# Expert blocks of 128 rows instead of 256, their first layer in 16-bit halves that are prepared earlier, and resident biases

## The chip, the cores and the metric

One Trainium2 chip, one of its cores. The time is the device time of one execution in microseconds (us), as the median of the runs of one kernel. The engines are TensorE (PE, whose weight loads are listed as PEld), VectorE (DVE), ScalarE (ACT), GpSimd (POOL) and SyncE (SP, which here only issues DMAs and passes waits on).

## The reference

2500 nodes of 512 features pass a graph layer and then a layer of eight experts. Cut to what matters:

```python
x = x + gnn(_layernorm(x), edge_index)     # relu((h + segment_sum(h[src])) @ W1 + b1) @ W2 + b2
xt = _layernorm(x)
gate = softmax(xt @ Wg); topv, topi = top_k(gate, 2); topv = topv / (sum(topv) + 1e-06)
for e in range(8):                         # D = 512, H = 256
    h = gelu(xt @ W1[e] + b1[e])
    ye = h @ W2[e] + b2[e]
    out = out + ye * scores[:, e]          # scores is topv at the two chosen experts, else 0
x = x + out
```

All is float32. The node count, 80000 edges, and 2 experts for each node give 5000 (node, expert) rows for the experts.

## The kernel before

**Aggregation (to about 396 us).** The sum over edges is a matmul of node features with a matrix of edge counts. DVE builds one-hot rows for each of 125 windows of 20 nodes (`one_hots`: `hot_key`, `hot_lo`), PE multiplies them (`window`), ACT copies the counts out (`take_counts`), and PE multiplies the counts with the 16-bit halves of the features (`sums_tile`). An outer loop `for it in range(1, G + 1)` takes 25 windows a turn and lays in between them the second graph layer of an earlier group of 500 nodes (`mlp2` on PE; `logits_of`, `residual` and `residual_end` on DVE; `std2` on ACT; on POOL the low halves of the hidden rows and the sum of residual input and bias, `x_res`). DVE may be at most RING = 4 windows ahead of PE. All of it is one hand-written order per engine, in which every wait is on a semaphore. `residual_end` writes the normalised rows `xt` as float32, SP stores them to `xt_d` in DRAM.

**Routing (about 413 to 442 us).** DVE works out for each (node, expert) row a slot, so that each expert's rows fill whole blocks of B rows; PE spreads node numbers and scores over the slots. Experts hold different numbers of rows, so there are empty places. NB is the most blocks that there can be, and blocks behind the last real one are run through the same loops on all engines but PE, with rows that go to spare lines of the output.

**Blocks (from about 442 us).** POOL fetches each block's rows by indirect DMA (`gather`, 128 rows of 2 KB each) into one of XB places. PE turns them (`turn`, matmuls with an identity), ACT and DVE make the high and the low part of the turned rows (`turned_high`, `turned_low`; one buffer `xT_hi`, `xT_lo`), PE runs the first layer as three products (high by high, high by low, low by high), in two halves m of the 256 hidden columns; ACT applies Gelu with the bias (`he`), DVE makes the low half (`he_lo`), PE runs the second layer, again three products; DVE adds the expert's second bias (`y`), ACT multiplies by the score, POOL adds the rows to the output by an indirect DMA that accumulates (`add_rows`). In the source the order for block k is the same on each engine: on ACT Gelu of k, the turned rows of k + 1, then the score of k; on DVE `he_lo` of k, turned rows of k + 1, then `y` of k.

An accumulating DMA must not run beside another that touches the same output row. Rows of one expert are all different nodes, so SP's `let_add` holds POOL's adds back only where the expert changes: there it waits until the last adds have landed. For the first YB blocks it waits on every earlier one. SP also loads the expert's second bias for each block (`load_bias`).

Each expert's weights W1, W2 are loaded as float32 and split by ACT (`split_high`) and DVE (`split_low`) into high and low parts, partly before the blocks and partly in their first rounds.

Counted from the reference with its own inputs, the experts get 407, 291, 1018, 356, 656, 1545, 405 and 322 rows.

## Time and profile before

| what | value |
|---|---|
| median of 3 runs | 638.52 us (637.46 to 639.03) |
| the profiled execution's own time | 639.89 us |
| its span (first to last instruction shown) | 638.1 us |
| busy, share of the span | PE 87%, DVE 66%, ACT 48%, POOL 40% |
| granted TensorE clock, mean | 0.948 of full speed |
| matmuls of each kind in the experts' first layer | 192, that is 24 blocks of 8 |

The shares are means over three stages that differ: how full each engine is in the stage that a change touches is read from the table of stretches, and what ends last there from the order of instructions in time.

### The profile page before, as it was taken

Reading aid. Unit: us, or ns where it says so; the run is one execution under the profiler, and the core shown is the slowest. Engines: PE = TensorE matmul, PEld = TensorE weight load, DVE = VectorE, ACT = ScalarE, POOL = GpSimd, SP = SyncE. Lnnn points to the kernel's source line nnn. Section 1 sums busy time; section 2 is a strip of 40 time slices with the busy share of each in tenths; the row PEclk is TensorE's granted clock in tenths of the full one; section 3 lists DMA queues with packets and bytes.
Section 4 is the critical chain, followed back from the end, with each engine's and each line's share of the span. In section 5 each row is a group of like instructions: output and inputs, shape, how many; then the busy total and the mean of one; then the engine's idle time right before and its main releaser. Section 6 shows DMA issues by size and latency. Waiting matters only on the chain.

```text
span 638.1 us, 10741 instructions
## 1 busy us (share of the span) xinstructions
PE 555.6 (87%) x3852; PEld 437.3 (69%) x3853; DVE 419.2 (66%) x802; ACT 307.9 (48%) x582; POOL 252.2 (40%) x222
## 2 busy tenths in 40 slices
PE   5788879999999999999999999726999999999900
PEld 3688879667566666766766665725899998889800
DVE  4777888975588769867974321887766765545541
ACT  3464767442242251225222301658777776677761
POOL 4362323130080016004200610017567778788763
PEclk9999999999999999999999999956999999999965
DMA  8253300300021201310311132978678988999895
GB/s 254 86 146 95 104 1 1 77 1 1 2 65 49 85 15 49 97 50 3 96 51 50 50 97 66 336 251 263 134 167 181 191 187 191 192 209 187 178 183 67
DMA packets 40302, 71.91 MB, mean 113 GB/s; under 512 B 10313, under 2 KB 14545, under 8 KB 39714
## 3 DMA queue, kind: packets, MB, share of 16 engines
q0 software_dynamic: 12704, 29.22, 23.1%
q1 hardware_dynamic: 26103, 36.06, 19.0%
q10 hardware_dynamic: 1442, 5.94, 3.3%
q8 instruction: 32, 0.52, 0.3%
q14 instruction: 21, 0.17, 0.1%
HBM read 46.07 MB, written 26.69 MB: 114 GB/s over the span
## 4 chain that ended last, share of the span: by engine, by line
PE 53%; DMA 12%; POOL 10%; DVE 8%; ACT 7%; issue 6%; SPq 1%; ACTq 0%; POOLq 0%; DVEq 0%
PE psum L1429 27%; PE psum L1413 9%; PE psum L1466 7%; PE psum L1343 6%; POOL out_x L605 6%; DMA out_x<-y,target_i 6%; POOL xg L598 3%; DMA xg<-xt_d,token_i 2%; DMA b_now<-in_L_ffn_b 2%; DMA src_i<-in_src 2%; PE psum L1321 1%; ACT y L833 1%; DVE hot_key L1054 1%; DVE stat L867 1%; DVE hot_lo L1054 1%
## 5 line engine op out<-in xcount | busy, mean ns | idle before, releaser
L1054 DVE TENSOR_TENSOR hot_key<-iota_key,key_w 128x1200 f16<-128x1200 f16 x125 | 109.0, 872 | 48.7 <-PE psum L1413 47.8
L667 ACT ACTIVATE counts<-psum 128x400 bf16<-128x400 f32 x125 | 62.0, 508 | 155.9 <-PE psum L1413 155.7
L1429 PE MATMUL psum<-counts,z_hi 125*128 125x500 bf16 x400 | 101.8, 375 | 2.2 <-ACT h L691 1.6
L605 POOL DMA_INDIRECT out_x<-y,target_i x54 | 87.7, 1624 | 35.4 <-ACT y L833 12.8
L1429 PE MATMUL psum<-counts,z_lo 125*128 125x500 bf16 x400 | 101.5, 376 | 0.0
L570 POOL TENSOR_TENSOR h_lo<-h,h_hi 128x500 fp32r<-128x500 f32 x16 | 23.5, 1498 | 168.8 <-ACT h_hi L698 168.8
L1413 PE MATMUL psum<-hot_key,hot_lo 128*128 128x200 f16 x750 | 82.8, 250 | 4.9 <-DVE hot_lo L1054 3.5
L1054 DVE TENSOR_TENSOR hot_lo<-iota_lo,lo_w 128x768 f16<-128x768 f16 x125 | 84.5, 676 | 0.0
L1413 PEld LDWEIGHTS psum<-hot_key,hot_lo 128*128 128x128 f16 x750 | 66.0, 98 | 25.3 <-issue 5.3
L1429 PEld LDWEIGHTS psum<-counts,z_lo 125*128 125x128 f16 x400 | 39.3, 98 | 45.7 <-issue 1.1
L598 POOL DMA_INDIRECT xg<-xt_d,token_i x54 | 58.0, 1074 | 31.2 <-issue 16.2
L1268 DVE TENSOR_TENSOR he_lo<-he,he_hi 128x256 fp32r<-128x256 f32 x54 | 23.0, 426 | 64.6 <-ACT he L826 64.6
L1429 PEld LDWEIGHTS psum<-counts,z_hi 125*128 125x128 f16 x400 | 37.7, 98 | 30.2 <-SPq L447 1.9
L1562 PE MATMUL psum<-xT_hi,w_hi 128*128 128x256 f32 x192 | 54.3, 283 | 0.3 <-DVE xT_lo L1250 0.3
L1562 PE MATMUL psum<-xT_hi,w_lo 128*128 128x256 f32 x192 | 54.3, 283 | 0.0
L1562 PE MATMUL psum<-xT_lo,w_hi 128*128 128x256 f32 x192 | 54.3, 283 | 0.0
L833 ACT ACTIVATE y<-y,slot_score 128x512 f32<-128x512 f32 x54 | 36.0, 714 | 33.2 <-DVE y L1277 33.2
L573 POOL TENSOR_TENSOR x_res<-x_res,b_row 125x512 f32<-125x512 f32 x20 | 29.4, 1490 | 49.3 <-DMA x_res<-in_x 49.3
L557 POOL TENSOR_TENSOR z_lo<-z,z_hi 125x512 f16<-125x512 f32 x20 | 27.5, 1382 | 50.7 <-ACT z L660 50.7
L1573 PE MATMUL psum<-w_hi,he_hi 128*128 128x512 f32 x96 | 40.0, 416 | 3.2 <-DVE he_lo L1268 3.1
L1277 DVE TENSOR_TENSOR y<-psum,b_now 128x512 f32<-128x512 f32 x54 | 34.7, 684 | 10.1 <-DMA b_now<-in_L_ffn_b 6.6
L1466 PE MATMUL psum<-W_hi,h_hi 128*125 128x264 f32 (+1 forms) x128 | 37.9, 296 | 0.0
(259 smaller groups left out, 1149.6 us busy)
## 6 DMA issues: line engine op xcount, KB each, us to landing
w_raw<-in_L_ffn_W SPq DMA_DIRECT2D x16, 512.0 KB, 6.9
b_now<-in_L_ffn_b SPq DMA_DIRECT2D x27, 256.0 KB, 5.0
x_res<-in_x SPq DMA_DIRECT2D x20, 224.0 KB
out_x<-x SPq DMA_DIRECT2D x20, 224.0 KB
xt_d<-xt SPq DMA_DIRECT2D x20, 224.0 KB
W_raw<-in_L_gnn_W ACTq DMA_DIRECT2D x2, 1024.0 KB, 5.6
out_x<-in_x SPq DMA_DIRECT2D x1, 1536.0 KB, 9.5
x_in<-in_x ACTq DMA_DIRECT2D x3, 448.0 KB
```

Of the source, the lines that this page charges most:

```text
L598: pool.indirect_dma_start(out=xg[:, k % XB, i], out_offset=None, in_=xt_d[:, :], in_offset=bass.IndirectOffsetOnAxis(ap=token_i[:, 2 * k + ...
L605: pool.indirect_dma_start(out=out[:, :], in_=y[:, k % YB, i], in_offset=None, out_offset=bass.IndirectOffsetOnAxis(ap=target_i[:, 2 * k + ...
L667: act.activation(counts[:, it % 2, :, place:place + W], psum[:, WIN + w % 2, 0:MW].rearrange("p (w h) -> p h w", w=W), ACT.Copy).then_inc( ...
L833: act.activation(y[:, k % YB, i], y[:, k % YB, i], ACT.Copy, scale=slot_score[:, 2 * k + i:2 * k + i + 1])\
L1054: ins = dve.tensor_tensor(hot[:, w % RING].rearrange("p s (n two) -> p s n two", two=2), iota[:].rearrange("p (o n two) -> p o n two", o=1 ...
L1277: dve.tensor_tensor(y[:, k % YB, i], psum[:, 4 + i], b2_now[:, k % 2], ALU.add).then_inc(taken, 1)
L1343: ins = mm(psum[0:P, AGG + 2 * (t % 2) + b, 0:columns.stop - columns.start], x_[:, t % 2, k * P:(k + 1) * P], w_[:, k, columns], start=(n ...
L1413: ins = mm(psum[:, WIN + w % 2, a * MH:(a + 1) * MH], hot_lo[:, w % RING, k], hot_key[:, w % RING, k], start=(k == 0), stop=(k == SL - 1))
L1429: ins = mm(psum[:, AGG + c, 0:GN], half[:, t, c * 128:(c + 1) * 128], counts[0:P, g % 2, t], start=(t == 0 and n == 0), stop=(t == T - 1 a ...
L1466: ins = mm(psum[0:P, bank + b, 0:columns.stop - columns.start], h_[:, k, rows], w_[:, k, columns], start=(k == 0 and n == 0), stop=(k == K ...
L1562: ins = mm(psum[:, 2 + m, 0:B], w_[e][:, c, cols], x_[:, c], start=(c == 0 and i == 0), stop=(c == KC - 1 and i == 2))
L1573: ins = mm(psum[:, 4 + i, :], h_[:, m, i * 128:(i + 1) * 128], w_[e][:, m], start=(m == 0 and n == 0), stop=(m == HC - 1 and n == 2))
```

## The change

- B is 128 instead of 256. NB, by its formula, is 47 instead of 27. By the row counts above there are 4, 3, 8, 3, 6, 13, 4 and 3 = 44 blocks with rows (before 2, 2, 4, 2, 3, 7, 2 and 2 = 24), so 3 empty ones in both kernels.
- The rows `xt` are stored as two float16 halves, 1024 float16 a row, as many bytes as before. DVE (for the last five tiles ACT) writes the whole row and its high half, and POOL subtracts (`low_rows`); the store waits for POOL. `turn` now multiplies the gathered halves with a float16 identity, so ACT's copy `x_now` is gone, and the two halves of the turned rows are plain copies.
- W1 of each expert is scaled by powers of two, split into float16 halves and written to `up_d` in DRAM inside the third and fourth turn of the aggregation loop (it = 2 and 3, `up_slot`): per expert ACT makes sizes (`up_sizes`) and the high half (`up_high`), PE sums the sizes (`up_sums`), DVE scales (`up_scales`) and makes the low half (`up_low`). The loads and stores are on ACT's queue. The blocks' loading then takes both halves with one DMA, and only W2 is split there.
- Eight DMAs load all second biases (`b2_all`) before the blocks; ACT and DVE wait for them before block 0. `load_bias` is gone.
- Gelu is computed once for each half m; DVE copies the high part (`he_hi`) and subtracts.
- YB = 6 places for `y` of 128 rows instead of 3 of 256, XB = 8 places for gathered rows instead of 3 of 256. POOL puts `add_rows(k)` ahead of `gather(k + 8)`; before, a gather stood ahead of the add.
- The node numbers are spread by one table of 48 columns instead of two of 56; ACT's part in it is gone.

```diff
-B = 256
+B = 128
...
-XB = 3
-YB = 3
-PAD = 2 * YB * 128
-AHEAD = 5
+XB = 8
+YB = 6
+PAD = YB * 128
+AHEAD = 6
...
+        def up_slot(it, j, late=0):
+            turn, left = divmod(WG * (it - 2) + j - late, WG)
+            n = 4 * turn + (left - 7) // 5
+            return n if it >= 2 and left >= 7 and (left - 7) % 5 == 0 and 0 <= n <= NE else None
...
-                sp.dma_start(w1_raw[e][:], eW1[e].rearrange("(k p) h -> p k h", p=128)).then_inc(ew_in[e], 16)
+                sp.dma_start(w1_both[e][:], up_d[e]).then_inc(ew_in[e], 16)
...
+            for e in range(NE):
+                sp.dma_start(b2_all[:, e], eb2[e:e + 1, :].broadcast_to([128, D])).then_inc(S["eb_in"], 16)
...
+                if k == YB:
+                    sp.wait_ge(S["slots_known"], LANDINGS)
+                if k >= YB:
+                    landed = {a: sp.value_load(landed_i[0:1, a, k:k + 1], min_val=16, max_val=16 * NB)
+                              for a, back in ((0, 1), (1, YB - 1)) if k - back >= YB}
+                for back in range(1, YB):
+                    if k - back >= YB:
+                        sp.wait_ge(y_out[(k - back) % YB], landed[0 if (k - back) // YB == (k - 1) // YB else 1])
+                    elif k >= back:
+                        sp.wait_ge(y_out[(k - back) % YB], 16)
                 sp.sem_inc(S["rows_free"], 1)
...
+            def low_rows(g, q):
+                n = 4 * g + q
+                pool.wait_ge(S["xt_hi_ready"], n + 1)
+                pool.tensor_tensor(xt[:, q, 1], xt_whole[:, n % 2], xt[:, q, 0], ALU.subtract).then_inc(S["xt_ready"], 1)
...
             def add_rows(k):
                 pool.wait_ge(S["rows_free"], k + 1)
-                for i in range(2):
-                    pool.wait_ge(S["y_scaled"], 2 * k + i + 1)
-                    pool.indirect_dma_start(out=out[:, :], in_=y[:, k % YB, i], in_offset=None,
-                                            out_offset=bass.IndirectOffsetOnAxis(ap=target_i[:, 2 * k + i:2 * k + i + 1], axis=0),
-                                            compute_op=ALU.add).then_inc(y_out[k % YB], 16)
+                pool.wait_ge(S["y_scaled"], k + 1)
+                pool.indirect_dma_start(out=out[:, :], in_=y[:, k % YB], in_offset=None,
+                                        out_offset=bass.IndirectOffsetOnAxis(ap=target_i[:, k:k + 1], axis=0),
+                                        compute_op=ALU.add).then_inc(y_out[k % YB], 16)
...
+                act.wait_ge(S["xt_ready"], n - 1)
+                for part in (xt_whole[:, n % 2], xt[:, q, 0]):
+                    ins = act.activation(part, x2[:, q], ACT.Identity, scale=rstd2[:, n:n + 1], bias=ln2[:, q % 2, 9:10])
+                ins.then_inc(S["xt_hi_ready"], 1)
...
+            def up_high(e):
+                act.wait_ge(S["up_scaled"], 2 * e + 1)
+                if e >= 1:
+                    act.wait_ge(S["up_out"], 16 * e)
+                act.activation(up_split[:, 0], up_raw[:, e % 2], ACT.Copy).then_inc(S["up_rounded"], 1)
+            def next_up(e):
+                if e >= 1:
+                    act.wait_ge(S["up_scaled"], 2 * e)
+                    act.dma_start(up_d[e - 1], up_split[:]).then_inc(S["up_out"], 16)
+                if e + 1 < NE:
+                    load_up(e + 1)
...
-            act.wait_ge(S["at_tile_ready"], 1)
-            act.activation(token_part[:, :, 0], at_tile[:], ACT.Copy, scale=iota_p[:]).then_inc(S["parts_ready"], 1)
...
+            act.wait_ge(S["eb_in"], 16 * (NE + 1))
+            act.wait_ge(S["slots_known"], BLOCKS)
+            act.wait_ge(S["slots_known"], SCORES)
             for k in range(NB):
                 expert = act.value_load(expert_i[0:1, k:k + 1], min_val=0, max_val=NE - 1)
                 for m in range(HC):
                     act.wait_ge(S["up_done"], HC * k + m + 1)
                     if k >= 1:
                         act.wait_ge(S["he_ready"], HC * (k - 1) + m + 1)
-                    if k >= 1:
-                        act.wait_ge(S["down_done"], 2 * k)
-                    for half in (he_hi[:, m], he[:, m]):
-                        ins = act.activation(half, psum[:, 2 + m, 0:B], ACT.Gelu, bias=eb1_col[:, bass.ds(expert * HC + m, 1)])
-                    ins.then_inc(S["gelu_ready"], 1)
+                    at = bass.ds(expert * HC + m, 1)
+                    act.activation(he[:, m], psum[:, 2 + m, 0:B], ACT.Gelu, bias=eb1_col[:, at], scale=up_undo[:, at]).then_inc(S["gelu_ready"], 1)
                 turned_high(k + 1)
                 if k + 2 <= NB:
                     take_block(k + 2)
-                for i, taken in enumerate((S["y0_taken"], S["y1_taken"])):
-                    act.wait_ge(taken, k + 2)
-                    act.activation(y[:, k % YB, i], y[:, k % YB, i], ACT.Copy, scale=slot_score[:, 2 * k + i:2 * k + i + 1])\
-                       .then_inc(S["y_scaled"], 1)
+                act.wait_ge(S["y_taken"], k + 2)
+                act.activation(y[:, k % YB], y[:, k % YB], ACT.Copy, scale=slot_score[:, k:k + 1]).then_inc(S["y_scaled"], 1)
...
-                dve.tensor_scalar(xt[:, q], x2[:, q], ln2[:, q % 2, 6:7], rstd2[:, n:n + 1],
-                                  ALU.subtract, ALU.mult).then_inc(S["xt_ready"], 1)
+                if n >= 2:
+                    dve.wait_ge(S["xt_ready"], n - 1)
+                for part in (xt_whole[:, n % 2], xt[:, q, 0]):
+                    ins = dve.tensor_scalar(part, x2[:, q], ln2[:, q % 2, 6:7], rstd2[:, n:n + 1], ALU.subtract, ALU.mult)
+                ins.then_inc(S["xt_hi_ready"], 1)
...
+            def up_scales(n):
+                dve.wait_ge(S["up_summed"], n + 1)
+                if n < NE:
+                    dve.tensor_scalar(up_inverse[:], psum[:, SM, 0:H], LEAST, None, ALU.max).then_inc(S["up_read"], 1)
+                if n >= 1:
+                    dve.tensor_scalar(up_undo[:, HC * (n - 1):HC * n].bitcast(I32), psum[:, SM, H:H + HC].bitcast(I32),
+                                      -1, (254 - UP) << 23, ALU.mult, ALU.add).then_inc(S["up_read"], 1)
+                if n < NE:
+                    dve.wait_ge(S["up_read"], 2 * n + 1)
+                    step(dve.tensor_scalar(up_inverse[:].bitcast(I32), up_inverse[:].bitcast(I32), EXPONENT, EXPONENT,
+                                           ALU.bitwise_xor, ALU.bitwise_and))
+                    dve.tensor_tensor(up_raw[:, n % 2], up_raw[:, n % 2],
+                                      up_inverse[:].rearrange("p (o h) -> p o h", o=1).broadcast_to([128, KC, H]), ALU.mult)\
+                       .then_inc(S["up_scaled"], 1)
+            def up_low(e):
+                dve.wait_ge(S["up_rounded"], 2 * e + 2)
+                dve.tensor_tensor(up_split[:, 1], up_raw[:, e % 2], up_split[:, 0], ALU.subtract).then_inc(S["up_scaled"], 1)
...
-            split_low_up(0)
-            split_low_down(0)
-            split_low_up(1)
+                dve.wait_ge(S["turned"], 2 * k + 2)
+                dve.tensor_copy(xT_lo[:].rearrange("p c n -> p (c n)"), psum[:, 1]).then_inc(S["xT_ready"], 1)
+            split_low(0)
+            split_low(1)
...
+            dve.wait_ge(S["eb_in"], 16 * (NE + 1))
             for k in range(NB):
+                expert = dve.value_load(expert_i[0:1, k:k + 1], min_val=0, max_val=NE - 1)
                 for m in range(HC):
                     dve.wait_ge(S["gelu_ready"], HC * k + m + 1)
                     if k >= 1:
-                        dve.wait_ge(S["down_done"], 2 * k)
+                        dve.wait_ge(S["down_done"], k)
+                    step(dve.tensor_copy(he_hi[:, m], he[:, m]))
                     dve.tensor_tensor(he_lo[:, m], he[:, m], he_hi[:, m].bitcast(F32), ALU.subtract).then_inc(S["he_ready"], 1)
                 turned_low(k + 1)
-                if k < 2 * NE - 3:
-                    (split_low_down, split_low_up)[k % 2](1 + (k + 1) // 2)
-                dve.wait_ge(b2_in[k % 2], 16 * (k // 2 + 1))
+                if 2 <= k < NE:
+                    split_low(k)
                 if k >= YB:
-                    dve.wait_ge(y_out[k % YB], 32 * (k // YB))
-                for i, taken in enumerate((S["y0_taken"], S["y1_taken"])):
-                    dve.wait_ge(S["down_done"], 2 * k + i + 1)
-                    dve.tensor_tensor(y[:, k % YB, i], psum[:, 4 + i], b2_now[:, k % 2], ALU.add).then_inc(taken, 1)
+                    dve.wait_ge(y_out[k % YB], 16 * (k // YB))
+                dve.wait_ge(S["down_done"], k + 1)
+                dve.tensor_tensor(y[:, k % YB], psum[:, 4], b2_all[:, bass.ds(expert, 1)].rearrange("p o d -> p (o d)"), ALU.add).then_inc(S["y_taken"], 1)
...
+            def turn(k, place):
+                pe.wait_ge(S["x_now_ready"], k)
+                for h in range(2):
                     for c in range(KC):
-                        ins = pe.transpose(psum[:, i, c * 128:(c + 1) * 128], rows[:, i, c * 128:(c + 1) * 128], ident[:])
+                        rows = xg[:, place, h, c * 128:(c + 1) * 128]
+                        ins = mm(psum[:, h, c * 128:(c + 1) * 128], rows if place == 0 else rows.rearrange("p o d -> p (o d)"), ident16[:], start=True, stop=True)
...
-                    trio = [(w1_hi, xT_hi), (w1_lo, xT_hi), (w1_hi, xT_lo)]
+                    trio = [(0, xT_hi), (1, xT_hi), (0, xT_lo)]
                     for m in range(HC):
                         cols = slice(m * 128, (m + 1) * 128)
                         for c in range(KC):
-                            for i, (w_, x_) in enumerate(trio):
-                                ins = mm(psum[:, 2 + m, 0:B], w_[e][:, c, cols], x_[:, c], start=(c == 0 and i == 0),
+                            for i, (half, x_) in enumerate(trio):
+                                ins = mm(psum[:, 2 + m, 0:B], w1_both[e][:, half, c, cols], x_[:, c], start=(c == 0 and i == 0),
                                          stop=(c == KC - 1 and i == 2))
                         ins.then_inc(S["up_done"], 1)
-                    turn(k + 1)
+                    turn(k + 2, bass.ds((k + 1) & (XB - 1), 1))
                     trio = [(he_hi, w2_hi), (he_hi, w2_lo), (he_lo, w2_hi)]
                     for m in range(HC):
                         pe.wait_ge(S["he_ready"], k * 2 + (m + 1))
-                        for i in range(2):
-                            if m == 0:
-                                pe.wait_ge((S["y0_taken"], S["y1_taken"])[i], k + 1)
-                            for n, (h_, w_) in enumerate(trio):
-                                ins = mm(psum[:, 4 + i, :], h_[:, m, i * 128:(i + 1) * 128], w_[e][:, m],
-                                         start=(m == 0 and n == 0), stop=(m == HC - 1 and n == 2))
-                            if m == HC - 1:
-                                ins.then_inc(S["down_done"], 1)
+                        if m == 0:
+                            pe.wait_ge(S["y_taken"], k + 1)
+                        for n, (h_, w_) in enumerate(trio):
+                            ins = mm(psum[:, 4], h_[:, m], w_[e][:, m], start=(m == 0 and n == 0), stop=(m == HC - 1 and n == 2))
+                    ins.then_inc(S["down_done"], 1)
```

The order of DVE in the fourth turn of the aggregation loop, around one tile of `residual` and `residual_end` (`logits` to `ln` is the residual part, `hot_key` and `hot_lo` are one window's one-hot rows). Before:

```order
L1066 TENSOR_TENSOR logits<-psum,gate_in 125x8
L1068 MAX top<-logits 125x8
L1070 MAX_INDEX topi<-top,logits 125x8
L1079 TENSOR_TENSOR x<-psum,x_res 125x512
L1081 BN_STATS ln<-x 125x6
L1082 BN_AGGR ln<-ln 125x2
L1054 TENSOR_TENSOR hot_key<-iota_key,key_w 128x1200
L1054 TENSOR_TENSOR hot_lo<-iota_lo,lo_w 128x768
L1087 RECIPROCAL rstd<-ln 125x1
L1093 TENSOR_SCALAR xt<-x,ln,rstd 125x512
```

The same place in the changed kernel, on DVE again:

```order
L1114 TENSOR_TENSOR logits<-psum,gate_in 125x8
L1115 MAX top<-logits 125x8
L1116 MAX_INDEX topi<-top,logits 125x8
L1125 TENSOR_TENSOR x<-psum,x_res 125x512
L1127 BN_STATS ln<-x 125x6
L1128 BN_AGGR ln<-ln 125x2
L1162 TENSOR_TENSOR up_split<-up_raw,up_split 128x1024
L1102 TENSOR_TENSOR hot_key<-iota_key,key_w 128x1200
L1102 TENSOR_TENSOR hot_lo<-iota_lo,lo_w 128x768
L1133 RECIPROCAL rstd<-ln 125x1
L1142 TENSOR_SCALAR xt_whole<-x,ln,rstd 125x512
L1142 TENSOR_SCALAR xt<-x,ln,rstd 125x512
```

One subtraction of 1024 columns and a second normalised copy have come in. Three windows ahead of each such place DVE has this in the changed kernel, the scaling of one expert's W1:

```order
L1102 TENSOR_TENSOR hot_key<-iota_key,key_w 128x1200
L1102 TENSOR_TENSOR hot_lo<-iota_lo,lo_w 128x768
L1148 TENSOR_SCALAR up_inverse<-psum 128x256
L1150 TENSOR_SCALAR up_undo<-psum 128x2
L1154 TENSOR_SCALAR up_inverse<-up_inverse 128x256
L1156 TENSOR_TENSOR up_raw<-up_raw,up_inverse 128x1024
```

Before, nothing stood between the one-hot rows there. The second place is ACT's round of one block. Before (`TENSOR_LOAD` and `ISA` are register work, here the block's expert and the address of its bias):

```order
L818 TENSOR_LOAD expert_i
L818 ISA x2
L826 ISA
L826 ACTIVATE he_hi<-psum,eb_col 128x256
L826 ACTIVATE he<-psum,eb_col 128x256
L826 ISA
L826 ACTIVATE he_hi<-psum,eb_col 128x256
L826 ACTIVATE he<-psum,eb_col 128x256
L801 ACTIVATE xT_hi<-psum 128x4x128 x2
L810 ACTIVATE x_now<-xg 128x1024
L833 ACTIVATE y<-y,slot_score 128x512 x2
```

ACT's round of one block in the changed kernel:

```order
L871 TENSOR_LOAD expert_i
L871 ISA x2
L877 ISA
L877 ACTIVATE he<-psum,eb_col,up_undo 128x128
L877 ISA
L877 ACTIVATE he<-psum,eb_col,up_undo 128x128
L855 ACTIVATE xT_hi<-psum 128x512
L882 ACTIVATE y<-y,slot_score 128x512
```

The round is shorter, and the score of block k still stands ahead of Gelu of block k + 1.

## Rows read from the trace of the kernel before

**Rows 1.** Windows: busy us (and instructions) per engine in five stretches, granted clock, DMA.
```profile
175.00:233.00 58.00, 55.97 (x380) 36.69 (x378) 44.83 (x77) 17.26 (x36) 12.98 (x8) 1.00 0.20 59
233.00:291.50 58.50, 58.50 (x409) 40.09 (x407) 46.51 (x86) 17.86 (x37) 12.35 (x8) 1.00 0.18 54
413.00:442.50 29.50, 10.05 (x90) 9.30 (x90) 26.65 (x70) 20.54 (x25) 12.20 (x20) 0.54 0.85 261
487.00:598.00 111.00, 107.76 (x713) 97.75 (x713) 63.46 (x105) 79.57 (x146) 86.87 (x65) 1.00 0.91 191
604.50:638.00 33.50, 0.20 (x1) 0.00 (x0) 11.04 (x20) 14.84 (x28) 16.98 (x12) 0.58 0.76 129
```

**Rows 2.** Page, the chain that ended last, by engine.
```profile
PE 53%; DMA 12%; POOL 10%; DVE 8%; ACT 7%; issue 6%; SPq 1%; ACTq 0%; POOLq 0%; DVEq 0%
```

**Rows 3.** Timeline, two rounds of blocks: start, duration, engine, idle before and releaser.
```profile
591.17 1.29 DVE L1277 TENSOR_TENSOR y<-psum,b_now 128x512 f32<-128x512 f32 x2 [0.29 <-PE psum L1573]
...
591.89 1.34 ACT L833 ACTIVATE y<-y,slot_score 128x512 f32<-128x512 f32 x2 [0.91 <-DVE y L1277]
...
593.29 0.47 ACT L826 ACTIVATE he_hi<-psum,eb_col 128x256 fp32r<-128x256 f32 x1
...
593.66 0.47 ACT L826 ACTIVATE he<-psum,eb_col 128x256 f32<-128x256 f32 x1
...
594.16 0.42 DVE L1268 TENSOR_TENSOR he_lo<-he,he_hi 128x256 fp32r<-128x256 f32 x1 [1.70 <-ACT he L826]
...
601.71 0.47 PE L1573 MATMUL psum<-w_hi,he_hi 128*128 128x512 f32 x1
...
603.63 0.39 PE L1573 MATMUL psum<-w_hi,he_lo 128*128 128x512 f32 x1
...
604.16 1.29 DVE L1277 TENSOR_TENSOR y<-psum,b_now 128x512 f32<-128x512 f32 x2 [0.29 <-PE psum L1573]
```

**Rows 4.** Timeline of DVE and PE, routing to the first block's `y`.
```profile
427.03 3.92 PE L1526 MATMUL psum<-token_part,at_row 125*128 125x112 f16 x40 [8.89 <-ACT token_part L788]
437.44 1.22 DVE L1142 TENSOR_TENSOR w_lo<-w_raw,w_hi 128x1024 fp32r<-128x1024 f32 x1
449.55 1.28 DVE L1277 TENSOR_TENSOR y<-psum,b_now 128x512 f32<-128x512 f32 x2
```

**Rows 5.** Timeline, three rows of the empty blocks at the end.
```profile
615.23 0.47 ACT L826 ACTIVATE he_hi<-psum,eb_col 128x256 fp32r<-128x256 f32 x1 [0.63 <-issue]
...
618.52 1.28 DVE L1277 TENSOR_TENSOR y<-psum,b_now 128x512 f32<-128x512 f32 x2
...
624.21 1.28 DVE L1277 TENSOR_TENSOR y<-psum,b_now 128x512 f32<-128x512 f32 x2
```

**Rows 6.** Groups by line and shape: busy us, mean ns, idle before.
```profile
L605 POOL DMA_INDIRECT out_x<-y,target_i x54 | 87.7, 1624 | 35.4 <-ACT y L833 12.8 <-issue 11.6 <-SPq L481 11.0
L598 POOL DMA_INDIRECT xg<-xt_d,token_i x54 | 58.0, 1074 | 31.2 <-issue 16.2 <-DVE token_i L1220 15.0
```

**Rows 7.** Timeline of POOL: two adds across a held-back place, and the last.
```profile
461.47 1.59 POOL L605 DMA_INDIRECT out_x<-y,target_i  x1 [0.30 <-issue]
...
467.60 1.63 POOL L605 DMA_INDIRECT out_x<-y,target_i  x1 [1.92 <-SPq L481]
...
628.27 1.55 POOL L605 DMA_INDIRECT out_x<-y,target_i  x1 [0.30 <-issue]
```

**Rows 8.** DVE's groups from 175 to 291.5 us.
```profile
L1054 DVE TENSOR_TENSOR hot_key<-iota_key,key_w 128x1200 f16<-128x1200 f16 x50 | 43.2, 864 | 21.6 <-PE psum L1413 21.6
L1054 DVE TENSOR_TENSOR hot_lo<-iota_lo,lo_w 128x768 f16<-128x768 f16 x50 | 36.0, 721 | 0.0
```

**Rows 9.** Timeline of DVE, one window's `hot_key` and `hot_lo` alone, one `hot_lo` beside POOL.
```profile
233.24 0.78 DVE L1054 TENSOR_TENSOR hot_key<-iota_key,key_w 128x1200 f16<-128x1200 f16 x1 [1.79 <-PE psum L1413]
233.94 0.55 DVE L1054 TENSOR_TENSOR hot_lo<-iota_lo,lo_w 128x768 f16<-128x768 f16 x1
...
241.87 1.59 DVE L1054 TENSOR_TENSOR hot_lo<-iota_lo,lo_w 128x768 f16<-128x768 f16 x1
```

361 lines of the change are left out of this document (189 added, 172 removed).

## The prediction

> **What bounds the kernel now.** I read the table of stretches first, since the shares of the page are means over stages. Up to 291.5 us PE is full, or nearly, and DVE busy for 44.8 and 46.5 us of 58 and 58.5 [rows 1]: the aggregation goes at PE's pace with DVE 20% below it. In routing PE is busy for 10 of 29.5 us at a granted clock of 0.54: DVE's small operations set that stage. In the blocks PE is busy for 107.8 of 111 us, POOL for 86.9 plus 0.30 us in front of each of its instructions. Behind 604.5 us PE does nothing and 33.5 us go by. The chain that ended last agrees: PE 53%, then DMA and POOL [rows 2].
>
> The timeline of the blocks shows more than the shares. From one `y` (591.17) to that two blocks later (604.16) are 13.0 us, 6.5 a block of 256 rows [rows 3]. Inside it runs a chain that closes on itself: `y` on DVE at 591.17, the score on ACT at 591.89, Gelu at 593.29, `he_lo` at 594.16, and only then can the second layer of the next block begin, which releases the next `y`. This chain is almost as long as PE's own work, so PE is full, but not alone in setting the pace. POOL is third: an add costs 1.62 + 0.30 us and a gather 1.07 + 0.30 [rows 6], 3.3 a pair and 6.6 for 256 rows.
>
> **The change part by part.** All against the profiled execution: span 638.1 us, its own time 639.9, the median of the runs 638.5.
>
> *PE's work in a block.* The spread of the node numbers runs 40 matmuls of 112 float16 columns in 3.92 us, 98 ns each, in the stretch of the half clock [rows 4]; at full clock 128 columns at 2.4 GHz are 53 ns, so the price of a first-layer matmul lies between 53 and 98. Near 60, 24 of them and 8 turning ones make 1.9 us; the second layer is 6 of 0.24 (eight steps from 601.71 to 603.63, [rows 3]) or 1.4. Together 3.3 us for 128 rows, where 3.25 were needed before: 16-bit halves of 128 columns save next to nothing against float32 at 256 columns, because two matmuls take the place of one.
>
> *The closed chain at 128 rows.* The order on ACT keeps the score of block k ahead of Gelu of k + 1, and PE's second layer of k + 1 needs that Gelu. Link by link: `y` to score 0.72 (591.17 to 591.89, same size as before). Score 0.67 (half of 1.34). Gelu to DVE: 0.50 at 256 columns (593.66 to 594.16); ACT's 512 columns cost 0.67 and 256 cost 0.37 (593.29 to 593.66), so 128 columns fewer take off about 0.12: 0.38. DVE now copies and subtracts, one behind the other: 0.42 at 256 and 0.645 at 512 columns give about 0.31 at 128, twice, plus 0.08 of hand-over: 0.70. Second layer: five steps of 0.24 and 0.53 from the last start to `y` (603.63 to 604.16): 1.73 [rows 3]. Sum 4.2. ACT also fetches the expert's number between score and Gelu; in the empty blocks Gelu starts 0.63 us late for "issue" [rows 5], behind 591.89 it starts at once, as two scores hid it and now there is one. I take 0.18, bounds 0 and 0.45. So 4.4 us a block (4.2 to 4.65). PE's 3.3 and POOL's 3.3 lie below it, and PE will be busy for about three quarters.
>
> *The blocks.* Before, 449.55 [rows 4] to 604.16 [rows 3], first `y` to last, are 154.6 us for 23 steps. Now there are 43 steps: 43 x 4.4 = 189. The split of W2 stands ahead of `y` on DVE in blocks 2 to 7: from Gelu, 0.38 + 2 x 0.62 + 0.65 (turned rows) + 1.22 [rows 4] = 3.5, against 2.8 for the second layer, 0.7 late six times: 4 us. Together 193, or **+38.5** (30 to 49).
>
> *POOL and the adds.* A held-back add starts 6.1 us behind the one before it [rows 7]. Blocks 1 to 6 are held by the fixed rule and block 7 by a change of expert, then blocks 15, 18, 24, 37, 41 (from the row counts). Seven times 6.1 against 4.4 put POOL 12 us, under three blocks, behind; there are six places, so DVE's wait on `y_out` does not bite, and at 3.3 a pair it catches up. Gathers queued behind a held add are eight blocks ahead. Cost nothing; the cover is that 4.4 is above 3.3.
>
> *The aggregation loop.* In its third and fourth turn DVE gets, for each of 8 experts, two operations of 256 columns (0.42 each, [rows 3]), two of 1024 (1.22, as `w_lo`, [rows 4]) and a small one, 3.5 with gaps: 28 us. Seven second copies of the normalised rows add 0.65 each, as `y` has for 512 columns [rows 3]: 4.6. POOL gets seven subtractions of about 1.5. A window's `hot_lo` takes 0.55 alone and 1.59 beside POOL's work [rows 9], so part of POOL's 10.5 shows up on DVE; DVE's 50 `hot_key` and `hot_lo` take 43.2 + 36.0 = 79 us [rows 8]; alone they would be 50 x (0.70 + 0.55) = 62 (233.24 to 233.94 to its end, [rows 9]); POOL is busy for 25 us in the two turns [rows 1], so 0.7 for each us of POOL: 7. Together 39.6 us. Idle there is 25.2 (116.5 less 91.3, [rows 1]), 21.6 of it waits for PE's window [rows 8]. So DVE runs out, by 14.5 us. The lead of up to four windows covers some, but `up_sums` now waits for a `residual` that stands two windows ahead, and `mlp2` for `up_scales` likewise: two windows, 2.3 us each, are left: about **+11**. Not below +5: eight times four matmuls of 256 columns (0.11 each) and two tiny ones are on PE, 0.65 us an expert. Not above +18.
>
> First the row: beside POOL the one-hot row is 1.04 us longer. The Trainium skill, page "SBUF — State Buffer", section "SBUF: two separate sides", says that the port pair shared by VectorE and GpSimd is locked for a whole instruction and the loser fully blocks. By that rule all 10.5 us of the new subtractions come off DVE, and the sum would be 3.5 us higher.
>
> *Routing.* DVE loses 1.22 (one split fewer before the blocks) and about 0.8 on narrower tables; PE no longer waits for ACT's part of the spread, but the scores' chain on DVE covers most of that. Turning and the first half of the first layer are shorter, so the first `y` comes about 5 us earlier. Against it, the residual input of the last group is now loaded behind a store that waits for POOL's subtraction, 1.5. **-3.5** (-5 to +1). The upper end is the biases: eight DMAs queued on SP behind the last experts, with DMAs at 0.85 of their time there [rows 1], and both ACT and DVE wait for all of them.
>
> *The tail.* Empty blocks come 5.7 us apart (618.52 to 624.21, [rows 5]); from the last `y` at 604.16 to the end are 33.9. Now an empty round on ACT and DVE alone is 0.72 + 0.67 + 0.45 + 0.38 + 2 x 0.62 + 0.65 = 4.1, three of them 12.3, then 1.55 to the last add and 9.8 from its start to the end (628.27 to 638.1, [rows 7]): 23.7, **-10.2** (-12 to -8).
>
> Sum: 11 - 3.5 + 38.5 - 10.2 = +35.8, a span near 674 us. On the median that is **674 us**, since 638.5 + 35.8 = 674.3.
>
> **The rivals.**
> *POOL or PE sets the blocks* (0.12). If the chain is under 3.9, the adds do: 7 x 6.1 + 31 x 3.3 + 5 x 1.9 + 15 for five changes of expert = 170, a total of 651. For it: POOL's rows are exact and the links are scaled by slope. Against it: the same links account for the 6.5 us of before. PE by its rows is no bound here. The Trainium skill, page "TensorE: Matmul & The Clock Gate", section "Back-to-back issue gap", gives about 81 ns a matmul for a stream of weight loads and matmuls at N = 128; by it PE would need 4.0 a block, and this case would end near 657.
>
> *The preparation costs more* (0.12). Each expert passes ACT, PE, DVE, ACT, DVE and the queue in turn, and ACT's `up_high` waits for the store of the expert before. ACT is busy for 17 of 58 us, which speaks against; but its counts are queued behind these waits, and PE waits for counts. At 2.5 us more an expert, 20 in all: 694.
>
> *The clock falls* (0.03). With PE idle for a quarter of a block the granted clock could drop from 1.00 in the blocks to half, as it stands at 0.54 in routing. Second layer 1.2 us longer, 5.6 a block: 726. In the first stretches of the blocks it stayed at 1.00 with small gaps.
>
> *Faster* (0.05). The place is the chain: if Gelu of k + 1 does not really wait for the score of k, blocks go at 3.3 and the phase is 142 plus landings that fewer DMAs shorten. The total passes 638 where a block costs under 3.55 and an add lands within 4.5 us. Near 630. The listed order speaks against it.
>
> *It evens out* (0.03): 638.
>
> **How the numbers follow.** My forecast, the closed chain at 4.2 to 4.65, has 0.65 and by the ends of its terms 656 to 697. The range 650 to 697 adds the POOL case and part of the costly preparation, and leaves out 0.2. Slower by over 0.3% (what the runs' spread can tell from none) are the forecast and three rivals, 0.92; faster 0.05; same 0.03.
>
> **What would show it.** `y` to `y` 4.4 us in the changed kernel's blocks, Gelu released by "issue" or DVE and not by PE; PE's second layer waiting for `he_lo`, PE busy near 75%; POOL idle for ACT's `y` from block 15 on. Turns three and four of the aggregation at 62 to 66 us instead of 58.3, with DVE above 95%. A last `y` some 24 us before the end. I am wrong if `y` to `y` is near 3.3, or the two turns keep their length.

## The result, and the profile after

The median went from 638.77 us (637.46 to 644.35, 4 runs) to **698.31 us** (696.54 to 698.59, 4 runs): 1.091 times the time of before, 95% interval 1.084 to 1.098. The profiled execution took 698.51 us, with a span of 696.4. 674 was forecast, with a range up to 697: the sign and the main mechanism were right, the size was 24 us short, and the measured time lies 1.3 us above the range.

The page of the changed kernel, first the engines, then the chain that ended last [rows 2]:

```profile
PE 561.5 (81%) x4532; PEld 424.0 (61%) x4533; DVE 461.8 (66%) x969; ACT 280.5 (40%) x539; POOL 278.8 (40%) x230
...
PE 49%; DVE 24%; ACT 9%; issue 6%; SPq 4%; DMA 4%; ACTq 2%; DVEq 1%; POOL 1%; POOLq 0%
```

The chain's share of DVE went from 8 to 24% though DVE is no busier in the mean: DVE's small steps now stand between PE's. The stretches of the changed kernel (busy us and instructions of PE, PEld, DVE, ACT, POOL, granted clock, DMA share, GB/s) are the two turns with the preparation, routing, the first eight blocks, the others, and the tail:

```profile
177.60:241.50 63.90, 61.08 (x419) 41.20 (x419) 59.49 (x100) 25.28 (x46) 25.98 (x14) 1.00 0.40 119
241.50:306.00 64.50, 63.42 (x441) 43.35 (x440) 60.92 (x111) 25.36 (x46) 25.39 (x12) 1.00 0.33 106
410.00:472.00 62.00, 28.26 (x251) 25.13 (x250) 39.95 (x117) 26.58 (x40) 19.16 (x27) 0.68 0.73 249
472.00:513.40 41.40, 29.60 (x308) 24.08 (x307) 24.25 (x55) 16.22 (x32) 20.68 (x16) 0.95 0.50 90
513.40:673.70 160.30, 121.84 (x1328) 99.28 (x1326) 80.14 (x210) 70.72 (x140) 86.34 (x67) 1.00 0.61 110
673.70:696.40 22.70, 0.00 (x0) 0.00 (x0) 7.86 (x19) 6.76 (x13) 6.21 (x4) 0.59 0.40 56
```

One block of the changed kernel on the timeline, from `y` to `y`, as [rows 3] has two of before:

```profile
535.86 0.69 DVE L1341 TENSOR_TENSOR y<-psum,b_all 128x512 f32<-128x512 f32 x1 [0.86 <-PE psum L1652]
...
536.59 0.72 ACT L882 ACTIVATE y<-y,slot_score 128x512 f32<-128x512 f32 x1 [2.43 <-DVE y L1341]
...
536.84 0.61 PE L1619 MATMUL psum<-ident,xg 128*128 128x128 f16 x8
537.37 0.81 ACT L877 ACTIVATE he<-psum,eb_col,up_undo 128x128 f32<-128x128 f32 x2
537.86 0.23 DVE L1333 CAST he_hi<-he 128x128 fp32r<-128x128 f32 x1 [1.30 <-ACT he L877]
...
538.12 0.32 DVE L1334 TENSOR_TENSOR he_lo<-he,he_hi 128x128 fp32r<-128x128 f32 x1
...
538.49 0.50 PE L1652 MATMUL psum<-w_hi,he_hi 128*128 128x512 f32 x1 [1.05 <-DVE he_lo L1334]
...
539.76 0.40 PE L1652 MATMUL psum<-w_hi,he_lo 128*128 128x512 f32 x1
...
540.06 0.28 PE L1642 MATMUL psum<-xT_hi,w_both 128*128 128x128 f16 x2
...
540.38 0.69 DVE L1341 TENSOR_TENSOR y<-psum,b_all 128x512 f32<-128x512 f32 x1 [0.87 <-PE psum L1652]
```

`y`, score, Gelu, `he_hi`, `he_lo`, second layer, `y`: 4.52 us (4.50 in most blocks), and PE stands still for the 1.05 us ahead of 538.49 although its first layer and its turning were done. The chain of the forecast is there, link by link.

By stages the span grew by 58.3 us. The sum of a group of nodes ends with one matmul of PE's (L1506; before L1442), which marks the turns:

| stage | before | after | change | forecast |
|---|---|---|---|---|
| to the mark before the turns with the preparation | 173.8 | 176.3 | +2.5 | 0 |
| the aggregation's turns | 58.5, 58.6, 58.55 | 62.9, 64.5, 59.7 | +11.5 | +11 |
| the last group's sums, to PE's last mark | 46.0 | 46.0 | 0 | 0 |
| end of the aggregation (first hidden rows of the last group on ACT) to the first `y` | 53.7 | 62.1 | +8.4 | -3.5 |
| first to last real `y` | 154.6 | 201.7 | +47.1 | +38.5 |
| last real `y` to the end | 33.9 | 22.7 | -11.2 | -10.2 |

The 0.4 us between that mark and the first hidden rows is left out. The first line is scatter: in the twelve experiments, whose edits all act behind it, PE's mark lies between 171.4 and 175.7.

### The profile page after: what moved, and what is told of

Same layout as the page of the kernel before. It is cut to its first block, busy times and chain, and to the rows that moved or that the text cites. A ratio compares the mean times of both kernels' runs of the same rounds, so it can differ in the third digit from the quotient of the medians.

```text
span 696.4 us, 13316 instructions
## 1 busy us (share of the span) xinstructions
PE 561.5 (81%) x4532; PEld 424.0 (61%) x4533; DVE 461.8 (66%) x969; ACT 280.5 (40%) x539; POOL 278.8 (40%) x230
## 4 chain that ended last, share of the span: by engine, by line
PE 49%; DVE 24%; ACT 9%; issue 6%; SPq 4%; DMA 4%; ACTq 2%; DVEq 1%; POOL 1%; POOLq 0%
PE psum L1493 20%; PE psum L1652 9%; PE psum L1477 7%; PE psum L1532 5%; DVE y L1341 4%; PE psum L1407 4%; DVE hot_key L1102 4%; DVE hot_lo L1102 3%; ACT he L877 3%; ACT y L882 3%; DVE he_lo L1334 2%; DVE he_hi L1333 2%; SPq L487 2%; DMA src_i<-in_src 2%; ACTq L871 1%
## 5 line engine op out<-in xcount | busy, mean ns | idle before, releaser
L701 ACT ACTIVATE counts<-psum 128x400 bf16<-128x400 f32 x125 | 61.7, 507 | 155.1 <-PE psum L1477 155.0
L640 POOL DMA_INDIRECT out_x<-y,target_i x47 | 74.7, 1589 | 107.2 <-ACT y L882 70.8
L882 ACT ACTIVATE y<-y,slot_score 128x512 f32<-128x512 f32 x47 | 33.9, 722 | 115.2 <-DVE y L1341 112.8
L1333 DVE CAST he_hi<-he 128x128 fp32r<-128x128 f32 x94 | 22.5, 240 | 75.6 <-ACT he L877 75.6
L610 POOL TENSOR_TENSOR x_res<-x_res,b_row 125x512 f32<-125x512 f32 x20 | 34.8, 1746 | 86.0 <-DMA x_res<-in_x 86.0
L1642 PE MATMUL psum<-xT_hi,w_both 128*128 128x128 f16 x704 | 65.8, 222 | 2.9 <-DVE xT_lo L1315 2.7
L1642 PEld LDWEIGHTS psum<-xT_hi,w_both 128*128 128x128 f16 x704 | 53.5, 100 | 15.7 <-issue 11.9
L1642 PE MATMUL psum<-xT_lo,w_both 128*128 128x128 f16 x352 | 62.6, 222 | 0.0
L606 POOL TENSOR_TENSOR xt<-xt_whole,xt 125x512 f16<-125x512 f32 x20 | 43.1, 2156 | 45.6 <-DVE xt L1142 34.9
L1652 PEld LDWEIGHTS psum<-w_hi,he_hi 128*128 128x128 f32 x88 | 16.8, 191 | 67.6 <-DVE he_lo L1334 63.8
L634 POOL DMA_INDIRECT xg<-xt_d,token_i x47 | 47.0, 999 | 23.9 <-issue 14.0
L1341 DVE TENSOR_TENSOR y<-psum,b_all 128x512 f32<-128x512 f32 x47 | 32.4, 690 | 34.7 <-PE psum L1652 34.7
```

Of the source, the lines that this page charges most:

```text
L606: pool.tensor_tensor(xt[:, q, 1], xt_whole[:, n % 2], xt[:, q, 0], ALU.subtract).then_inc(S["xt_ready"], 1)
L634: pool.indirect_dma_start(out=xg[:, k % XB].rearrange("p a d -> p (a d)"), out_offset=None, in_=xt_d[:, :], in_offset=bass.IndirectOffsetO ...
L640: pool.indirect_dma_start(out=out[:, :], in_=y[:, k % YB], in_offset=None, out_offset=bass.IndirectOffsetOnAxis(ap=target_i[:, k:k + 1], a ...
L701: act.activation(counts[:, it % 2, :, place:place + W], psum[:, WIN + w % 2, 0:MW].rearrange("p (w h) -> p h w", w=W), ACT.Copy).then_inc( ...
L882: act.activation(y[:, k % YB], y[:, k % YB], ACT.Copy, scale=slot_score[:, k:k + 1]).then_inc(S["y_scaled"], 1)
L1333: step(dve.tensor_copy(he_hi[:, m], he[:, m]))
```

## The experiments

All numbers below are medians of the runs; each batch had its own runs of the kernel before, 638.6 to 640.8 us. Edits are to the changed kernel unless another is named.

### e1_bias: the first bias apart, the second ones as they are needed

```diff
+            sp.dma_start(eb1_col[:], ...).then_inc(S["eb_in"], 16)
             for e in range(AHEAD, NE):
                 load_expert(e)
             for e in range(NE):
-                sp.dma_start(b2_all[:, e], ...).then_inc(S["eb_in"], 16)
+                sp.dma_start(b2_all[:, e], ...).then_inc(b2_in[e][0], 16)
...
-            act.wait_ge(S["eb_in"], 16 * (NE + 1))
+            act.wait_ge(S["eb_in"], 16)
...
+                if k < NE:
+                    dve.wait_ge(b2_in[k][0], b2_in[k][1] + 16)
                 dve.wait_ge(S["down_done"], k + 1)
```

> The first bias has a semaphore of its own and is loaded ahead of experts 6 and 7; ACT waits for it alone, and DVE waits for the second bias of one more expert per block, right before y. Theory (the wait for all biases made the start 8.4 us late): without it Gelu of block 0 starts when the first layer is done, first y at 463 to 466 instead of 472.0, the blocks' length unchanged at 202, total 698.3 - 7 = 691 (689 to 694). Rival (the gathered rows or the loads of experts 6 and 7 set the start too): first y moves by 3 us or less, total 695 to 698.

Measured: 689.62 us (687.52 to 692.43); first `y` at 465.27, blocks 201.9. ACT around the first Gelu in the changed kernel, and in this one:

```profile
457.75 0.60 ACT L855 ACTIVATE xT_hi<-psum 128x512 f16<-128x512 f32 x1 [9.17 <-remote]
...
467.80 0.80 ACT L877 ACTIVATE he<-psum,eb_col,up_undo 128x128 f32<-128x128 f32 x2 [7.56 <-DMA b_all<-in_L_ffn_b]
```

```profile
460.03 1.06 ACT L742 ACTIVATE w_hi<-w_raw 128x1024 fp32r<-128x1024 f32 x1 [5.03 <-DMA w_raw<-in_L_ffn_W]
461.02 0.81 ACT L880 ACTIVATE he<-psum,eb_col,up_undo 128x128 f32<-128x128 f32 x2
```

The theory holds: the wait of 7.56 us for the biases is gone. What is late next is the load of W2 of the last expert, 5.03 us, whose split stands ahead of Gelu on ACT; so 57.5 us from the aggregation to the first `y` are left, against 62.1 in the changed kernel and 53.7 before. By this stage the edit is worth 4.6 us; of the other 4 us between the medians, 2.3 stand at the start of the trace (PE's mark at 174.0 against 176.3), which is scatter.

### e2_score_late: the score behind Gelu, out of the chain

```diff
                 turned_high(k + 1)
                 if k + 2 <= NB:
                     take_block(k + 2)
-                act.wait_ge(S["y_taken"], k + 2)
-                act.activation(y[:, k % YB], ..., scale=slot_score[:, k:k + 1]).then_inc(S["y_scaled"], 1)
+                if k >= 1:
+                    score(k - 1)
+            score(NB - 1)
```

> ACT scores block k-1 after Gelu and turned rows of block k instead of before Gelu of k. Theory (the closed chain y, score, Gelu, he, second layer sets the blocks at 4.5 us): the score leaves the chain, Gelu waits for PE's first layer instead. That layer started 0.32 us before y (540.06 against 540.38) and needs 12 x 0.056 + 0.28 to its half, so Gelu at about 541.0 instead of 541.9, y to y 3.6 to 3.7 instead of 4.5, total 698.3 - 31 to 37 = 661 to 667. Rival A (POOL's pairs or the landing of the adds set the pace): y to y stays at 4.5 or moves by 0.3 at most, total 688 to 699, and POOL no longer waits for ACT. Rival B (DVE sets it): y to y 4.0 to 4.2, total near 680.

Measured: **653.69 us** (651.30 to 655.21), 44.6 less than the changed kernel. One block here:

```profile
587.66 0.69 DVE L1346 TENSOR_TENSOR y<-psum,b_all 128x512 f32<-128x512 f32 x1 [0.63 <-PE psum L1657]
...
588.29 0.46 ACT L881 ACTIVATE he<-psum,eb_col,up_undo 128x128 f32<-128x128 f32 x1 [1.59 <-PE psum L1647]
...
588.78 0.23 DVE L1338 CAST he_hi<-he 128x128 fp32r<-128x128 f32 x1 [0.43 <-ACT he L881]
...
589.79 0.72 ACT L864 ACTIVATE y<-y,slot_score 128x512 f32<-128x512 f32 x1
...
591.28 0.69 DVE L1346 TENSOR_TENSOR y<-psum,b_all 128x512 f32<-128x512 f32 x1 [0.68 <-PE psum L1657]
```

3.62 us instead of 4.50. Gelu is now released by PE, and the score comes behind it. Over the stage PE's busy time tells the rest (the stretch from first to last real `y`, in this kernel and in the one before):

```profile
469.60:632.50 162.90, 152.35 (x1633) 121.02 (x1631) 109.60 (x264) 87.35 (x174) 108.13 (x81) 0.99 0.72 130
```

```profile
449.60:604.20 154.60, 151.36 (x1009) 137.68 (x1009) 91.62 (x152) 111.56 (x206) 116.90 (x87) 1.00 0.87 181
```

PE has the same 151 to 152 us of work in blocks of 128 and of 256 rows, and the changed kernel has them too (29.60 and 121.84 in the table above). The closed chain is shown as the cause of the slow blocks, and PE is what sets them once it is cut. The gain in the blocks, 38.8 us, was larger than the 31 to 37 expected, because the long blocks shrank too: the first eight steps from 5.2 to 3.8 us each. The empty blocks went from 4.13 to 2.5.

What made blocks long in the changed kernel stands in its sequencer's rows (the sequencer is the part of an engine that fetches values and waits). While the score of one block runs, ACT's sequencer fetches the expert's number of the next, and Gelu needs it:

```profile
L871 ACTq TENSOR_LOAD <-expert_i x43: 273/322/985, 472.7 to 669.6; - x43
```

These are least, median and most in ns, over the blocks from 472 to 673.7 us. In 28 of the 43 steps the fetch took some 0.3 us and was over before the score, and Gelu followed the score at once. In blocks 2 to 8, 17, 20, 26, 34, 36, 38 and 43 it took 0.50 to 0.99 us, and there Gelu came 0.23 to 0.72 us behind the end of the score; with one more such gap in block 21 these are the idle times ahead of Gelu in the view of its line, L877 (us, times):

```profile
  PE psum L1642: 5.1, 9
  issue: 1.9, 6
```

The view puts 5.1 of these 7.0 us down to PE, but PE had ended its half of the first layer some 1 us before. Nearly the same blocks have the long fetch in e1, e3, e4 and e7. In e2 single fetches take up to 0.81 us as well, but they fall into the time in which Gelu waits for PE. What makes a fetch long isn't shown.

### e3_three_turns: three experts a turn instead of four

```diff
-            n = 4 * turn + (left - 7) // 5
-            return n if it >= 2 and left >= 7 and (left - 7) % 5 == 0 and 0 <= n <= NE else None
+            n = 3 * turn + (left - 7) // 5
+            return n if it >= 2 and 7 <= left < 22 and (left - 7) % 5 == 0 and 0 <= n <= NE else None
```

The place of `up_sums` between the other work of PE is adapted to three (`4 * g + 1 + n % 3`).

> The weights' preparation takes three experts a turn (it = 2, 3, 4) instead of four in it = 2 and 3. Theory (DVE runs out in the two turns; each has some 12 us of slack, and beyond it each us of work shows): three experts leave each turn 4 to 5 us less work, so the turns' growth of 5.3 and 6.0 us falls to 0.5 to 2 each and the third gets 0.5 to 2: total growth 3 to 5 instead of 11.5, total 698.3 - 7 = 691 (689 to 694). Rival (each expert costs a fixed time by hand-overs between ACT, PE and DVE, whatever the slack): growth stays 10.5 to 12, spread over three turns, total 697 to 699.

Measured: 695.75 us (694.80 to 698.56). The turns were 61.9, 62.8 and 61.7 us, a growth of 10.8 in place of 11.5, though DVE had three experts a turn and was idle for 5.2, 6.1 and 10.5 us of them. The growth is what the rival forecast: each expert costs 1.1 to 1.4 us in whatever turn it stands; the rival's reason, the hand-overs, is tested in e7. That DVE runs out falls. In the changed kernel PE was busy for 123.6 of the 127.5 us of the two turns and DVE for 118.6.

### e4_no_low: without POOL's subtraction

`low_rows` only signals, but for its first four calls, which set the rows' low half to zero (0.52 us each); this part of the computation is left out.

> POOL's subtraction for the low half of the stored rows is left out (the low half is zero, so that the output is that of rounded rows). Theory (POOL's 2.16 us each, seven in the two turns, slow DVE's one-hot rows): DVE's hot_key and hot_lo in these turns lose some 0.5 to 0.7 us for each us of POOL taken away, 15 us less of POOL is 7 to 10 us less of DVE, and the growth of 11.5 falls to 2 to 6; the stores of the last tiles are earlier, so the first y 1 to 3 us earlier: total 698.3 - 9 = 689 (686 to 693). Rival (the subtractions lie beside DVE at no cost, or PE sets the turns): growth 10 to 12, total 696 to 698.

Measured: 694.88 us (692.87 to 696.83). Turns of 63.25, 64.15 and 59.5, a growth of 11.2. DVE's busiest groups in the two turns, in the changed kernel and here (mean ns behind the busy us):

```profile
L1102 DVE TENSOR_TENSOR hot_key<-iota_key,key_w 128x1200 f16<-128x1200 f16 x51 | 45.9, 899 | 6.8 <-PE psum L1477 6.8
L1102 DVE TENSOR_TENSOR hot_lo<-iota_lo,lo_w 128x768 f16<-128x768 f16 x51 | 34.4, 674 | 0.0
...
L1154 DVE TENSOR_SCALAR up_inverse<-up_inverse 128x256 int32<-128x256 int32 x8 | 5.7, 712 | 0.3
```

```profile
L1105 DVE TENSOR_TENSOR hot_key<-iota_key,key_w 128x1200 f16<-128x1200 f16 x50 | 46.9, 937 | 7.8 <-PE psum L1480 7.8
L1105 DVE TENSOR_TENSOR hot_lo<-iota_lo,lo_w 128x768 f16<-128x768 f16 x50 | 35.0, 700 | 0.0
...
L1157 DVE TENSOR_SCALAR up_inverse<-up_inverse 128x256 int32<-128x256 int32 x8 | 2.4, 294 | 0.3
```

POOL was busy for 30.9 us in place of 51.4, and the one-hot rows did not become shorter by it. The theory missed, both in DVE's time and in the turns'. Only the first `y` came 2.7 us earlier behind the aggregation, as the stores wait less.

The single rows show why. A `hot_key` takes 0.78 or about 1.83 us and a `hot_lo` 0.55 or about 1.6, with almost nothing in between. Long ones are 12 in the two turns of the kernel before, 12 in the changed kernel and 15 here. First a place of the changed kernel, then one of this run:

```profile
277.24 0.77 DVE L1102 TENSOR_TENSOR hot_key<-iota_key,key_w 128x1200 f16<-128x1200 f16 x1
277.40 2.10 POOL L606 TENSOR_TENSOR xt<-xt_whole,xt 125x512 f16<-125x512 f32 x1 [4.55 <-DVE xt L1142]
...
278.92 0.73 DVE L1154 TENSOR_SCALAR up_inverse<-up_inverse 128x256 int32<-128x256 int32 x1
```

```profile
268.59 1.27 POOL L613 TENSOR_TENSOR x_res<-x_res,b_row 125x512 f32<-125x512 f32 x1 [9.66 <-DMA x_res<-in_x]
268.69 1.82 DVE L1105 TENSOR_TENSOR hot_key<-iota_key,key_w 128x1200 f16<-128x1200 f16 x1 [1.85 <-PE psum L1480]
```

In both places the one that starts second is the longer one, and all 39 long rows of the three runs start while an instruction of POOL is at work. Six of the seven subtractions in the two turns start 0.16 us behind a `hot_key`: the rows of DVE keep their length, and POOL's subtraction takes 2.1 us, one even 4.4, where it takes 1.15 with no one-hot row beside it (from 373 us on). In the third row of the first place, `up_inverse`, is DVE the later one; it ends 0.15 us behind POOL's. Leaving the subtractions out moved POOL's other additions, and some of these then started ahead of a one-hot row. So POOL mostly paid for the new subtractions, and POOL is not what the turns wait for.

### e7_no_undo: PE's share of the preparation

The main part of the edit; DVE's `up_undo` then reads other numbers, for all experts but the last.

```diff
-                    for m in range(HC):
+                    for m in range(HC if n == NE else 0):
                         ins = mm(psum[:, SM, H + m:H + m + 1], up_inverse[0:1, m * 128:(m + 1) * 128], ones[0:1], start=True, stop=True)
```

> The changed kernel without PE's 14 matmuls of one column in the preparation (two for each expert but the last), so that the factor by which Gelu's input is scaled back is taken from other numbers and the output is not the reference's. Theory (PE's own added work makes most of the aggregation's growth of 11.5 us; these two cost 0.53 us an expert, from 210.62 to 211.15): growth 11.5 - 7 x 0.53 = 7.8 (7 to 9), total 698.3 - 3.7 = 694.6. Rival (hand-overs between ACT, PE and DVE or DVE's load set the turns): growth 11 to 12, total 697 to 699.

Measured: 694.42 us (690.04 to 695.62); turns of 61.0, 62.1 and 59.9, a growth of 7.3 in place of 11.5. The theory holds: 4.2 us less, where 3.7 were expected. PE's own groups of the preparation in the changed kernel, from 177.6 to 306 us, and one of them on the timeline:

```profile
L1565 PE MATMUL psum<-up_abs,part 128*128 128x256 bf16 x32 | 4.9, 275 | 1.2 <-DVE ln L1128 1.2
L1561 PE MATMUL psum<-ones,up_inverse 1*128 1x1 f32 x28 | 4.2, 250 | 0.4 <-DVE ln L1128 0.4
```

```profile
210.62 0.60 PE L1561 MATMUL psum<-ones,up_inverse 1*128 1x1 f32 x4
...
211.15 0.61 PE L1565 MATMUL psum<-up_abs,part 128*128 128x256 bf16 x4
...
211.60 0.59 PE L1493 MATMUL psum<-counts,z_hi 125*128 125x500 bf16 x2
```

From 210.62 to 211.15 are 0.53 us for two products with a single column (four instructions in the trace), from there to 211.60 another 0.45 for the sums: 0.98 us an expert. Seven of these and one of 0.45 are 7.3 of the 10.3 us by which the first two turns grew; PE also idles there for 2.0 us on DVE: 1.6 ahead of these matmuls, as the rows say, and 0.4 ahead of `mlp2`, for `up_undo`. About 1 us is not accounted for.

### e6_before_score: the late score in the kernel before

The edit of e2 in the kernel before, 256 rows a block.

> The kernel before, with 256 rows a block, and only the score moved behind Gelu, as in e2_score_late. Theory (there PE was busy for 107.8 of 111 us in the blocks, so that the chain with the score in it was hidden behind PE): at most 3% of 155 us in the blocks comes off, 0 to 4.5 us, and up to 2 us in the empty blocks: total 633 to 640. Rival (the closed chain set the pace there as well, and the score, 1.34 us a block, comes off in 23 steps): 31 us off, total 608 to 615.

Measured: 646.58 us (642.16 to 649.62) against 640.80 beside it, 1.012 times (1.008 to 1.016). The rival, 31 us faster, is out: PE did hide that chain at 256 rows. But the theory's 633 to 640 was missed too: this kernel is 6 us slower, and its blocks take 159.1 us where they took 154.6. The waits in the blocks, first of this kernel, then of the one before (us in total, times, longest):

```profile
ACT x_now L810 <- DMA xg<-xt_d,token_i: 29.3, 17, 5.1
...
DVE y L1282 <- DMA b_now<-in_L_ffn_b: 14.8, 8, 3.3
DVE he_lo L1273 <- issue: 12.8, 7, 3.3
```

```profile
ACT x_now L810 <- DMA xg<-xt_d,token_i: 10.4, 8, 3.0
...
DVE y L1277 <- DMA b_now<-in_L_ffn_b: 4.2, 4, 1.9
```

A reading that fits, but that no run tests: a later score makes POOL's add late, and with three places for rows the gathers and, on SP, the bias of the block stand behind it. Eight places and resident biases loosen just this, so that this part of the change may be what lets e2 gain. How much of the 6 us is this coupling stays open: this run lay beside e5's, whose trouble (next) it may share in the 12.8 us of "issue".

### e5_all, e9, e10 and e11: the edits together

> The three edits e1_bias, e2_score_late and e3_three_turns together. If they act on places that don't overlap, their gains add: from 698.3 by 8.7, 44.6 and 2.6 to 642 by the medians, or by the stages of the traces (first y 4.7 earlier behind the aggregation, blocks 38.8 and tail 3.3 less, aggregation 0.7 less) to 698.5 - 47.5 = 651. Theory (additive, up to runs' spread): 642 to 651. Rival (the first y was covered by the long early blocks, or the bias now delays y of block 0 to 7): 652 to 655, with y to y over 4.2 in the first blocks.

Measured: 656.34 us (654.52 to 657.82): neither. The first `y` came 55.7 us behind the aggregation, but the blocks took 173.0 us. In e2 Gelu of the second half starts 0.32 to 0.33 us behind PE's turning in nearly every block; here it came 0.6 to 1.6 us behind in 21 of 40, with nothing in the trace that it waits for but the first layer, which had ended. One such place in this run, where Gelu starts 0.63 us behind the turning:

```profile
589.04 0.29 PE L1651 MATMUL psum<-xT_hi,w_both 128*128 128x128 f16 x2
...
590.39 0.61 PE L1628 MATMUL psum<-ident,xg 128*128 128x128 f16 x8
...
591.02 0.46 ACT L884 ACTIVATE he<-psum,eb_col,up_undo 128x128 f32<-128x128 f32 x1 [0.52 <-PE psum L1651]
```

So the kernels of e2 and e5 were run again, and one with two of the three edits.

> The kernel of e2_score_late once more, beside e10 and e11, since e5_all's blocks took 173 us where e2's took 163, with Gelu of the second half 0.3 us or more late in e5's trace and never in e2's. If that lateness belongs to the edit of the biases, this run repeats e2: 651 to 656, Gelu of the second half 0.33 us behind the start of PE's turning in every block. If it comes from where a run happens to be (another chip, another placement), this run may show it too: 660 or more.

> The kernel of e5_all once more. If the lateness of Gelu belongs to the kernel: 654 to 658, blocks 170 to 175 us. If it belonged to that run's place: 644 to 650, blocks near 163 us.

> e2 and e1 together, without the three turns of e3. If the biases' edit brings the late Gelu: 654 to 660, blocks 170 to 175. If the three turns bring it, or the place of the run: 645 to 650, blocks near 163 us, first y near 58 us behind the aggregation.

Measured: e9 651.62 us (651.23 to 657.33), e10 647.55 (643.58 to 649.33), e11 643.89 (642.04 to 650.63), with blocks of 163.1, 162.2 and 162.1 us, and no late Gelu of this kind in any of the three. The lateness belonged to where and when e5 ran, not to an edit: e10 is the same kernel, on another chip and in a later batch. Whether it was the chip, and what it is there, isn't shown. e11 is 1.012 times the kernel before (1.006 to 1.018): 54 of the 60 us are back, and it is still the slower one.

### e8_ahead and e12_ahead_again: the first layer one block ahead

```diff
-                with pe.Fori(start, end) as k:
...
+                with pe.If(end > start + 1):
+                    with pe.Fori(start + 1, end) as k:
+                        up(e, k, k & 1)
+                        turn(k + 2, bass.ds((k + 1) & (XB - 1), 1))
+                        down(e, k, (k + 1) & 1)
```

Only PE's loop is shown. `up` is the first layer of block k; `down`, whose semaphore counts are one block ahead, is the second layer of block k - 1. e8 has the three turns of e3, e12 has not.

> e5_all, and PE runs the first layer of block k+1 and turns k+2 ahead of the second layer of block k, with two banks for each sum, DVE takes the turned rows first and y one block later, ACT the score two blocks later. Theory (after the score, only PE's wait for he and its own work of 1.34 + 0.61 + 1.45 = 3.4 us a block are left): y to y 3.45 to 3.6 instead of 3.6 to 4.2, blocks 150 to 155 instead of 163, total 636 to 642. Rival A (POOL, at 3.17 a pair plus the waits for landed adds where the expert changes): y to y falls to no less than 3.6 and POOL has no idle but the landings, total 643 to 648. Rival B (DVE, whose copies slow down beside POOL from 0.23 to 0.5 us): y to y 3.8 to 4.0, total 648 to 654.

> e8_ahead without the three turns, that is e11_score_bias and PE's first layer one block ahead. e8's trace shows PE without a gap in blocks of 3.58 to 3.62 us, beside stretches with Gelu or the turned rows late as in e5's run at the same place. Theory (undisturbed, PE's own work sets the blocks, 3.6 us for 128 rows): blocks 43 x 3.6 to 3.7 = 155 to 159 instead of 162, the first y 5 to 7 us later, since PE does the first layer of block 1 before the second of block 0, and the tail unchanged: total 639 to 646 against 643.9 of e11, so no gain that counts over it and none over the kernel before. Rival (the gaps of e11, 0.2 to 0.6 us a block, all go, and the later first y is made up): 633 to 637, faster than before.

Measured: e8 656.05 us (654.87 to 659.37) on the chip of e5, with stretches of late Gelu as there, so that its expected 636 to 642 was missed and its stage of 167.9 us tells little; e12 649.18 (648.18 to 649.97), elsewhere, 1.016 times the kernel before (1.013 to 1.019). In e12 most blocks take 3.57 to 3.7 us and the stage 156.5 us where e11 had 162.1, as expected, but the first `y` comes 6.3 us later behind the aggregation and the end 2.8 us later behind the last `y`. Its profile also starts 4 us later than e11's, the scatter named above. The total missed the expected range by 3 us. PE was busy for 147.4 of the 156.5 us, so its work sets the blocks, and neither of the two orders tried beats the kernel before.

## Why the prediction was right, and where its sizes were off

- **The closed chain sets the blocks: right.** Its links were forecast at 4.38 us and measured at 4.52: score 0.73 (0.72), to Gelu 0.78 (0.85), to `he_hi` 0.49 (0.38), to PE 0.63 (0.70), to the next `y` 1.89 (1.73). The link to `he_hi` was off because Gelu's cost was scaled by columns alone: 128 columns take 453 ns on ACT where 256 took 468. But it isn't the same instruction: it now also reads its scale from a tile (`up_undo`). In the same trace an activation of 500 columns takes 769 ns with bias and scale from tiles (`h`) and 590 with neither (`xT_top`), an estimate of 0.09 us for each; so the second operand, which the sum left out, can have taken back the 0.1 us of the columns. No run separates the two. e2 shows the cause of the slow blocks, by cutting the chain.
- **Blocks, +38.5 against +47.1: the fetch and W2's split were mis-sized.** Most blocks took 4.50 us, and 43 of these are 193.5 of the 201.7. The other 8 are the fetch of the expert's number, 7.0 us of idle time ahead of Gelu in 15 blocks, and one block of 6.25 us in which the second layer went at 0.43 us a step instead of 0.23, at a granted clock of 0.55. The forecast had given the fetch an even 0.18 us a block, at most 0.45; it took nearly nothing in 28 steps and up to 0.72 in the others. The 4 us for W2's split in the early blocks came near by luck: these did cost 5.4 us more than 4.50 each, but `y` was only some 0.2 us late behind the split, and the rest was the fetch and the slow block.
- **PE's work for 128 rows is no less than before: right**, 151 us in all. A first-layer matmul took 56 ns at a granted clock of 1.00, near the 60 taken. The Trainium skill's 81 ns ("TensorE: Matmul & The Clock Gate", "Back-to-back issue gap") did not show in this stream.
- **Aggregation, +11 against +11.5, by a wrong step.** "DVE runs out, by 14.5 us" fell with e3 and e4: neither a lighter turn nor 20 us less of POOL moved it. What was named as the lower bound, PE's added work, is the cost, at 0.98 us an expert instead of 0.65 and with its waits; that the sum came within 0.5 us is luck, the more so as its own terms, 14.5 less two windows of 2.3, give 9.9 and not 11. The 7 us that DVE was to lose to POOL's subtractions were not there: as many one-hot rows were long as before. The prediction also weighed the Trainium skill ("SBUF — State Buffer", "SBUF: two separate sides") as if all of POOL's new work came off DVE. The page says that whichever of the two starts first keeps the shared pair for its whole instruction and the other blocks. The traces agree, 2.10 us for POOL's subtraction behind a `hot_key` against 1.15 alone; here the later one was mostly POOL.
- **Routing, -3.5 against +8.4: the step that failed.** The wait for all eight second biases was named as the upper end at +1 and cost 7.6 us at Gelu of block 0. It was in the diff: the loads are issued behind two experts at a time when DMAs are at their fullest. PE stood still meanwhile, and the second layer of block 0 then ran at a granted clock of 0.50. This one stage is half of the 24 us. Without that wait e1 still has +3.8, so the 5 us that the first `y` was to come earlier were not there either: the first layer of block 0 began 48.7 us behind the end of the aggregation, where it began 46.7 us behind it before. The store that waits for POOL, forecast at 1.5 us, cost 2.7 by e4; for the rest no run has the cause.
- **Tail, -10.2 against -11.2:** right; empty blocks 4.13 us apart, forecast 4.1.
- **POOL:** held-back adds stood 5.2 us apart, not 6.1, and the blocks show no wait for them, as forecast. At 3.6 us a block the cover is gone: in e2 an add lagged up to 15.6 us behind its `y`, and ACT waited 3.4 us for gathered rows.

The rival by which POOL or PE sets the blocks (12%) was wrong for this kernel and describes e2. The range's upper end, 697, was 1.3 us short; the upper ends of the forecast's own terms (49, 18, 1 and -8) add to 698.5, so that summed rightly they would have held the measured 698.3.

## What to carry to other kernels

Halving a tile halves an engine's work for each step but not the hand-overs between engines; write the closed chain of a step link by link, and compare it with the busiest engine at the new size before halving. When a chain closes through three engines, look in it for work that nobody in it needs (here the score, 0.7 us of 4.5) and move it behind: that was worth three quarters of the loss. When a load is made once for all, see what waits for the last of them. And look at the sequencer's rows of an engine in the chain: a fetch that is short in most rounds can be long in some.

## What the runs showed of the hardware

- Two products of one column each (float32, one row of 128 by one) cost PE 0.53 us, more than four of 256 columns in bfloat16 (0.45).
- DVE's one-hot rows are long (`hot_key` 1.83 us in place of 0.78, `hot_lo` 1.6 in place of 0.55) only where they start while an instruction of POOL is at work, 39 of 39 in three runs; a subtraction of POOL that starts 0.16 us behind a `hot_key` takes 2.1 us in place of 1.15.
- ACT's fetch of one number from a tile took 0.27 to 0.99 us in the changed kernel's blocks, median 0.32, and nearly the same blocks had the long ones in five kernels.
- DVE's copy `he_hi` of 128 columns takes 0.23 us, but 0.37 to 0.55 in all 13 places of e2 where it starts 0.56 to 0.72 us into POOL's issue of an add or a gather; started at other points of such an issue it mostly keeps its 0.23, and the subtraction behind it its 0.29:

```profile
573.63 1.58 POOL L640 DMA_INDIRECT out_x<-y,target_i  x1 [2.73 <-SPq L500]
...
574.29 0.46 DVE L1338 CAST he_hi<-he 128x128 fp32r<-128x128 f32 x1
574.78 0.29 DVE L1339 TENSOR_TENSOR he_lo<-he,he_hi 128x128 fp32r<-128x128 f32 x1
```

  Over gathers such a copy ends 1.03 us into the issue, over adds 1.04 to 1.14. Several of the blocks of 3.8 us among those of 3.6 in e2's second half have one. The exclusive-or on 256 integers took 712 ns in the mean beside POOL's subtractions and 294 in e4.
- One kernel gave 656.3 us on one chip and 647.6 on another, in another batch, while the kernel before moved by 2 us, through Gelus that start late for no cause in the trace.
